# A non-local block and two Mamba passes: the last 1x1 convolution of 20 of 28 position tiles inside the second Mamba stage, z made in its own tile, GpSimd's ring with five places

## What is computed

```python
def _mamba(u, in_w, conv_w, conv_b, xp_w, dt_w, dt_b, A_log, Dp, out_w):
    x, z = jnp.split(u @ in_w.T, 2, axis=-1)          # 512 channels each
    x = silu(depthwise_conv4(x) + conv_b)
    xdbl = x @ xp_w.T                                 # dt (16), B (16), C (16)
    dt = softplus(xdbl[..., :16] @ dt_w.T + dt_b)
    h_t = exp(dt * A) * h_(t-1) + (dt * x) * B        # 16 states for each of 512 channels
    y = (sum_n h * C + x * Dp) * silu(z)
    return y @ out_w.T
y1, y2 = mamba1(x0), mamba2(x0)                       # x0: result of layer 0
out = cat_conv_w @ concat(y1, y2) + cat_conv_b + x0
```

## Time and profile before

| | us |
|---|---|
| median of 3 runs | 6042.82 (6040.0 to 6043.99) |
| the profiled execution | 6041.77 |
| its span, first to last instruction | 6040.0 |
| PE busy | 5095.7 (84%) |
| DVE busy | 5052.4 (84%) |
| POOL busy | 5066.3 (84%) |
| ACT busy | 3549.0 (59%) |
| `finish`, first matmul to end of span | 5774.2 to 6040.0 |

### The profile page before, as it was taken

How to read it: one execution, slowest core, us unless ns; L and a number is a source line. 1 busy time by engine, 2 the same in 40 slices (tenths; PEclk the granted TensorE clock), 3 DMA queues, 4 the chain that set the end, 5 groups by cost and what they waited for, 6 DMA issues and landing times. The chain is left out here.

```text
span 6040.0 us, 69966 instructions
## 1 busy us (share of the span) xinstructions
PE 5095.7 (84%) x25566; PEld 3554.5 (59%) x25566; DVE 5052.4 (84%) x3473; ACT 3549.0 (59%) x5494; POOL 5066.3 (84%) x2582
## 2 busy tenths in 40 slices
PE   6968888888888888888678888888888888888789
PEld 5836565665565566555545566655665566665544
DVE  3459999999999999999949999999999999999900
ACT  0046666666666666666546666666666666666511
...
GB/s 153 70 101 100 94 76 108 68 98 100 71 108 68 99 100 70 108 68 98 59 76 100 104 66 107 64 103 90 80 108 62 104 82 87 108 62 101 56 212 143
DMA packets 220108, 563.74 MB, mean 93 GB/s; under 512 B 27794, under 2 KB 94226, under 8 KB 218228
## 3 DMA queue, kind: packets, MB, share of 16 engines
...
## 5 line engine op out<-in xcount | busy, mean ns | idle before, releaser
L868 POOL TENSOR_TENSOR dbx<-dtx,b_all 128x896 f32<-128x896 f32 x1792 | 3695.0, 2090 | 0.2
L708 ACT ACTIVATE mamba_ps<-dt,w 128x448 f32<-128x448 f32 x3584 | 2132.4, 629 | 1555.9 <-DVE hc L820 1288.7
L813 DVE TENSOR_TENSOR_SCAN mamba_ps<-mamba_ps,dbx 128x896 f32<-128x896 f32 x1232 | 2483.2, 2016 | 211.0 <-ACT mamba_ps L708 109.7
L661 PEld LDWEIGHTS mamba_ps<-ident,hc 128*112 128x112 f32 x14336 | 1782.6, 145 | 787.9 <-issue 390.3
L661 PE MATMUL mamba_ps<-ident,hc 128*112 128x128 f32 x14336 | 2043.7, 295 | 234.3 <-POOL hc L875 141.9
L820 DVE TENSOR_TENSOR hc<-mamba_ps,c_all 128x896 f32<-128x896 f32 x1232 | 1341.6, 1089 | 137.1 <-DVE mamba_ps L813 3.4
L875 POOL TENSOR_TENSOR hc<-hc,c_all 128x896 f32<-128x896 f32 x560 | 1166.7, 2083 | 226.0 <-DVE hc L813 223.5
L813 DVE TENSOR_TENSOR_SCAN hc<-mamba_ps,dbx 128x896 f32<-128x896 f32 x560 | 1128.6, 2015 | 117.9 <-ACT mamba_ps L708 117.9
L577 PE MATMUL mamba_ps<-u,w 128*128 128x448 f32 x1792 | 880.6, 621 | 387.7 <-DVE sz L802 298.3
L577 PEld LDWEIGHTS mamba_ps<-u,w 128*128 128x128 f32 x1792 | 337.9, 209 | 643.2 <-DVE sz L802 327.3
L586 PE MATMUL mamba_ps<-x,taps 128*128 128x448 f32 (+3 forms) x1792 | 704.5, 536 | 12.0 <-ACT x L722 12.0
...
## 6 DMA issues: line engine op xcount, KB each, us to landing
b_all<-bc_scratch SPq DMA_DIRECT2D x448, 448.0 KB, 5.8
c_all<-bc_scratch SPq DMA_DIRECT2D x448, 448.0 KB, 5.1
u<-u_scratch SPq DMA_DIRECT2D x56, 448.0 KB, 7.7
y_scratch<-ytok SPq DMA_DIRECT2D x56, 448.0 KB, 3.2
src<-y_scratch SPq DMA_DIRECT2D x56, 448.0 KB, 4.6
...
u_scratch<-ub ACTq DMA_DIRECT2D x28, 448.0 KB, 8.2
src<-in_x SPq DMA_DIRECT2D x28, 448.0 KB, 6.8
```

Source lines behind the costliest of these rows:

```text
L661: ins = nc.tensor.matmul(y_ps[j % 2][:, c * 128:(c + 1) * 128], hc[g][:, e * T + c * TCH:e * T + (c + 1) * TCH], ident[:, :], start=False, ...
L708: ins = nc.scalar.activation(decay[g % 2][:, e * T:(e + 1) * T], blk(dt[t % 2], j), ACT.Exp, scale=w[:, c:c + 1])
L813: nc.vector.tensor_tensor_scan(dst, h, dbx[n % BX_RING][:, :], 0.0, ALU.mult, ALU.add).then_inc(scan_done, 1)
L868: nc.gpsimd.tensor_tensor(view(dbx[n % BX_RING], 0, [[T, 2], [1, T]]), view(dtx[t % 2], j * T, [[0, 2], [1, T]]), view(b_all, 2 * g * T, [ ...
```

## The change

The items z0 to z3 leave the front: they are made in their own tile, in slots 0 to 5, and silu of z moves from slot 3 to slot 8. The x and convolution items of the next tile move back to make room, out1's copy moves from ACT slot 16 to 15 (ahead of the decays of slot 16), y2 from PE slot 30 to 29. `dtx` becomes one buffer instead of two, with a wait on dbx, and the dbx ring has five places instead of six.

Under tiles 36 to 55 the jobs of batches 0 and 1 and six of batch 2 run, one job a tile, in two pieces of 224 columns: items fa0, fa1 (one for each output half) and fb0, fb1. The pieces share one source buffer and one result buffer. SP loads piece a after the load of u, and piece b, followed by the store of piece a, inside the loads of the next tile's rows, behind `c_all` of group 2; the store of piece b is at the end of its step. `finish` keeps eight jobs, each with its own buffers; its maps are loaded one by one and not copied.

```diff
 SCHEDULE = {
-    "x0": (0, 1), "x1": (1, 2), "c0": (3, 5), "c1": (4, 6), "y3": (6, None), "x2": (7, 8), "x3": (9, 10), "c2": (10, 11),
-    "c3": (12, 13), "out0": (13, 14), "out1": (15, 16), "y0": (16, None), "xp": (18, 19), "dt0": (19, 20), "dt1": (20, 21),
-    "dt2": (21, 22), "dt3": (22, 23), "y1": (23, None), "z0": (24, 25), "z1": (26, 27), "z2": (27, 28), "z3": (28, 29),
-    "y2": (30, None),
+    "z0": (0, 1), "z1": (1, 2), "x0": (2, 3), "x1": (3, 4), "z2": (4, 5), "z3": (5, 6), "c0": (6, 7), "y3": (6, None),
+    "c1": (8, 9), "x2": (8, 10), "x3": (10, 11), "c2": (10, 12), "c3": (12, 13), "out0": (13, 14), "out1": (15, 15),
+    "y0": (16, None), "xp": (18, 19), "dt0": (19, 20), "dt1": (20, 21), "dt2": (21, 22), "dt3": (22, 23), "y1": (23, None),
+    "fa0": (24, 25), "fa1": (25, 26), "y2": (29, None), "fb0": (30, 31), "fb1": (31, 31),
 }
-FRONT = ("x0", "x1", "c0", "c1", "x2", "x3", "c2", "c3", "xp", "dt0", "dt1", "dt2", "dt3", "z0", "z1", "z2", "z3")
+FRONT = ("x0", "x1", "c0", "c1", "x2", "x3", "c2", "c3", "xp", "dt0", "dt1", "dt2", "dt3")
 BACK = ("y3", "out0", "out1")
-SILU_Z_AT, SILU_X_AT, SOFTPLUS_AT = 3, 16, 24
-TAKE_Y_AT = {3: 3, 12: 0, 20: 1, 28: 2}
+SILU_Z_AT, SILU_X_AT, SOFTPLUS_AT = 8, 16, 24
+TAKE_Y_AT = {4: 3, 12: 0, 20: 1, 28: 2}
 GATE_AT = {7: 3, 16: 0, 24: 1, 31: 2}
 DTX_AT, LATE_DTX_AT = {29: 0, 30: 1}, {6: 2, 7: 3}
 
 
+
+FIN, FIN_FROM = T // 2, TILES + TPB + 1
+FIN_TILES = range(FIN_FROM, 2 * TILES)
+
+
+def fin_of(t):
+
+    return (t - FIN_FROM) // TPB, (t - FIN_FROM) % TPB * T
+
+
 def due(engine, n):
 
     return [name for name, at in SCHEDULE.items() if at[engine] == n]
 
 
-BX_RING, HC_RING = 6, 8
+BX_RING, HC_RING = 5, 8
 
 
 def by_pool(n):
...
-        dtx = [sb(f"dtx{p}", DB * T) for p in range(2)]
+        dtx = sb("dtx", DB * T)
...
+                    b, n0 = fin_of(t)
+                    if piece == 1:
+                        it = Item(t, "fa1")
+                        sp.wait_ge(work_ready, it.ready())
+                    elif t > FIN_FROM:
+                        it = Item(t - 1, "fb1")
+                        sp.wait_ge(work_ready, it.ready())
+                    if piece == 0 and n0 == 0:
+                        if b:
+                            it = Item(t - 1, "fb1")
+                            sp.wait_ge(work_free[it.slot], it.freed())
+                        sp.dma_start(now[:, :], k_dram[b]).then_inc(now_ready, 16)
+                        sp.wait_ge(y_stored, 16 * (TILES + TPB * (b + 1)))
+                    n0 += piece * FIN
+                    s = src[:, :].rearrange("p (k n) -> p k n", k=6)
+                    for m in range(2):
+                        sp.dma_start(s[:, 2 * m:2 * m + 2, :], y_img[m][b][:, :, n0:n0 + FIN]).then_inc(src_ready, 16)
+                    sp.dma_start(s[:, 4:6, :], x_in[b].rearrange("(k p) n -> p k n", p=128)[:, :, n0:n0 + FIN]).then_inc(src_ready, 16)
+
+                def store_out(t, piece):
+                    b, n0 = fin_of(t)
+                    n0 += piece * FIN
+                    for oc in range(2):
+                        it = Item(t, f"f{'ab'[piece]}{oc}")
+                        sp.wait_ge(work_free[it.slot], it.freed())
+                    sp.dma_start(out[b].rearrange("(k p) n -> p k n", p=128)[:, :, n0:n0 + FIN],
+                                 res[:, :].rearrange("p (k n) -> p k n", k=2)).then_inc(out_stored, 16)
+
+                def between(t):
+                    if t in FIN_TILES:
+                        load_src(t, 1)
+                        store_out(t, 0)
 
                 def spread_bc(t):
...
+                        if g == 2:
+                            between(t - 1)
...
-                        sp.wait_ge(work_ready, Item(t, FRONT[-1]).ready())
+                        sp.wait_ge(work_ready, Item(t, "z3").ready())
                         load_u(t + 2)
+                    if t == FIN_FROM:
+                        sp.dma_start(cat_t[:, :], cat_dram).then_inc(cat_ready, 16)
+                    if t in FIN_TILES:
+                        load_src(t, 0)
                     if not first(t):
                         store(t - 1)
                     if last(t):
+                        between(t)
                         store(t)
                     else:
                         spread_bc(t + 1)
+                    if t in FIN_TILES:
+                        store_out(t, 1)
                 sp.wait_ge(y_stored, 2 * 16 * TILES)
...
+                def fin(t, piece, oc):
+                    if oc == 0:
+                        if t == FIN_FROM and piece == 0:
+                            pe.wait_ge(cat_ready, 16)
+                        pe.wait_ge(now_ready, 16 * (fin_of(t)[0] + 1))
+                        pe.wait_ge(src_ready, 48 * (2 * (t - FIN_FROM) + piece + 1))
+                    b = take(Item(t, f"f{'ab'[piece]}{oc}"))
+                    for k in range(6):
+                        m = cat_t[:, k * CH + oc * 128:k * CH + (oc + 1) * 128] if k < 4 else \
+                            now[:, (k - 4) * CH + oc * 128:(k - 4) * CH + (oc + 1) * 128]
+                        ins = nc.tensor.matmul(b[:, 0:FIN], m, src[:, k * FIN:(k + 1) * FIN], start=(k == 0), stop=(k == 5))
                     ins.then_inc(work_ready, 1)
 
...
+                            elif name[0] == "z":
+                                in_proj(t, name, DIN + int(name[1]) * 128)
+                            elif name[0] == "f":
+                                if t in FIN_TILES:
+                                    fin(t, "ab".index(name[1]), int(name[2]))
...
+                def take_fin(t, piece, oc):
+                    if oc == 0:
+                        upto(act, out_stored, 16 * (2 * (t - FIN_FROM) + piece))
+                    it = Item(t, f"f{'ab'[piece]}{oc}")
+                    nc.scalar.activation(res[:, oc * FIN:(oc + 1) * FIN], take(it)[:, 0:FIN], ACT.Identity,
+                                         bias=now[:, 2 * CH + oc:2 * CH + oc + 1]).then_inc(work_free[it.slot], 1)
...
+                    d, dx = pair(dt[t % 2], h), pair(dtx, h)
                     if k % 2 == 0:
                         pool.wait_ge(softplus_ready, t + 1)
+                        upto(pool, dbx_ready, SLOTS * (t - 1) + 16 * (h + 1))
...
+    b0, n0 = fin_of(2 * TILES)
+    jobs = [(b0, i) for i in range(n0 // T, TPB)] + [(b, i) for b in range(b0 + 1, BATCH) for i in range(TPB)]
...
-                dve.wait_ge(fixed, 32)
-                for b in range(BATCH):
-                    dve.wait_ge(made, b * TPB + TPB)
-                    dve.wait_ge(taken, b * TPB + TPB)
-                    nc.vector.tensor_copy(now[:, :], maps[:, bass.ds(b * KCOLS, KCOLS)]).then_inc(now_ready, 1)
```

More of the change, by code:

```diff
@@ L490, in mambas @@
             for name in SCHEDULE:
+                if name[0] == "f" and t not in FIN_TILES:
+                    continue
                 of = t + 1 if name in FRONT else t - 1 if name in BACK else t
@@ L904, in finish @@
         ps = ctx.enter_context(nc.psum_tensor("fin_ps", [128, 8 * 512], fp32))
-        src = [sb(f"src{i}", 6 * T) for i in range(TPB)]
-        res = [sb(f"res{i}", 2 * T) for i in range(TPB)]
-        cat_t, maps, now = sb("cat_tt", 4 * CH), sb("maps", BATCH * KCOLS), sb("now", KCOLS)
-        fixed, src_ready = sem("fixed"), [sem(f"src_ready{i}") for i in range(TPB)]
-        now_ready, made, taken = sem("now_ready"), sem("made"), sem("taken")
-        stored = [sem(f"out_stored{i}") for i in range(TPB)]
+        src = [sb(f"last_src{i}", 6 * T) for i in range(len(jobs))]
+        res = [sb(f"last_res{i}", 2 * T) for i in range(len(jobs))]
+        cat_t, maps = sb("last_cat", 4 * CH), [sb(f"map{b}", KCOLS) for b in batches]
+        fixed, src_ready = sem("fixed"), [sem(f"last_ready{i}") for i in range(len(jobs))]
+        made, taken, stored = sem("made"), sem("taken"), sem("last_stored")
         y_img = y_dram.rearrange("(m b t) n f -> m b (t n f)", m=2, b=BATCH).rearrange("m b (k p n) -> m b p k n", k=2, p=128)
@@ L936, in _ @@
+                for j, (b, i) in enumerate(jobs):
+                    s = src[j][:, :].rearrange("p (k n) -> p k n", k=6)
+                    for m in range(2):
+                        sp.dma_start(s[:, 2 * m:2 * m + 2, :], y_img[m][b][:, :, i * T:(i + 1) * T]).then_inc(src_ready[j], 16)
+                    sp.dma_start(s[:, 4:6, :], x_in[b].rearrange("(k p) n -> p k n", p=128)[:, :, i * T:(i + 1) * T]).then_inc(src_ready[j], 16)
             @block.tensor
             def _(pe):
-                pe.wait_ge(fixed, 32)
@@ L939, in _ @@
-                for b in range(BATCH):
-                    pe.wait_ge(now_ready, b + 1)
-                    for i in range(TPB):
-                        pe.wait_ge(src_ready[i], b * 48 + 48)
-                        back = 4 if i >= 4 else (7 if i == 3 else 3)
-                        pe.wait_ge(taken, b * TPB + (i + 1 - back + TPB))
-                        for oc in range(2):
```

(33 more changed lines are left out.)

64 lines of the change are left out of this document (26 added, 38 removed).

## The result

The changed kernel takes 6065.95 us (median of 5 runs, 6064.14 to 6071.32), the kernel before 6042.82 beside it (5 runs, 6037.19 to 6055.3). The ratio is 1.0038 [1.0024, 1.0053]: slower by 23 us. The forecast was 6085, slower by 42. The profiled execution has a span of 6063.2, 23.2 more than before.

A forecast was written before the change was run, and what follows sets the result against it. VectorE, waiting for ScalarE's decays, sets a tile's length; the last stage is TensorE alone. 6040.0 - 186.5 - 15.7 + 125 - 4 + 84 + 14 + 25 = 6082 us of span, forecast 6085, range 5950 to 6175.

The forecast's parts named there:

- Last stage: TensorE's closing stage shrinks from 28 jobs to 8, from 261.4 to 74.9 us: 186.5 saved.
- Lead-ins: ScalarE's four z copies leave the two lead-ins, where they stood between dt and softplus: 15.7 us saved.
- Part 3: z in slots 0 to 5 makes out1 late, its copy ahead of slot 16's decays: +2.4 us a tile, 125 over 52.
- The seam: First scan (S0) of the tile after each of tiles 36 to 54, late behind fb1: 4.4 us each, 84 over 19.
- The backlog: TensorE, still owing a sum and z0 behind a seam, is 0.8 us later than elsewhere: 14 us over 18.
- Tiles 0, 27, 28, 55: These tiles lack half of the delaying items and win the 1.0 us wait at slot 4: -4 us in all.
- Queue of SP, rows of B, ring of five, one dtx: Rows queued behind the pieces on SP (bounds 0 to 3), GpSimd's five-place ring (0 to 1 a tile), single dtx: 0 us.
- Clock: TensorE at half clock for dt makes softplus late: half of the 49 us if all tiles turn long, 25.
- A: TensorE's queue is absorbed, out1 there when ScalarE comes: Part 3 and Clock 0, 5935 us, or 6010 with half; chance 0.24.
- B: Half clock spreads to all tiles, fb1 and the next tile's x0: 87 us more, 6172, slower; chance 0.18.
- C: GpSimd starves, by group 3's rows or the ring: about 6140 us, slower; chance 0.08.

The follow-up runs named there:

- Experiment 1: The changed kernel with out1's copy back in ACT slot 16, behind that slot's decays: 5963.3 us, 0.9879 of the kernel before.
- experiment 9: The changed kernel with out1 made behind y0 in slot 17 and copied in slot 18, behind silu of x: 5751.65 us, 0.9526 of the kernel before.
- experiment 5: The changed kernel without pieces (all 28 jobs in the last stage) and with six ring places: 6189.23 us, against 6185.99 with five.
- experiment 8: The kernel before the change with idle transposes for TensorE in its two waits ahead of dt: 5914.71 us, 0.9782.
- experiment 11: The changed kernel with piece b's source loaded behind c_all of group 0 and piece a stored behind group 1: 6087.66 us, 1.0084 of the kernel before.
- experiments 6 to 8: Idle transposes (8 ahead of xp, 20 ahead of dt0) in the changed kernel, 5969.55 us; that with out1 at 16 and early fb pieces, 5829.62; the kernel before, 5914.71.

## Why the prediction was right, point by point

**Last stage.** 186.5 forecast, 185.7 measured; its matmuls take 74.37, forecast 74.9. **Lead-ins**: 15.7 forecast, 10.2 + 8.3 = 18.5 measured, the second with tile 27's gain of 0.8 in it.

**Part 3, the dear one.** Forecast +2.4 a tile; by slot it is -0.97 (slot 4) + 0.19 + 0.49 + 1.88 + 0.67 (slots 9, 15, 16, 17) = 2.26 in tiles 1 to 26, and 120 us over all 52, forecast 125. out1's matmuls end at 45.7, forecast 45.4 (44.23 + 1.2), and slot 17's scan starts at 53.0 in both. The path is the one named: ScalarE idle for out1 with slot 16's decays behind it. Experiment 1 shows it by giving these decays their place back, experiment 9 by taking out1 away altogether. What the prediction read as a term of 125 us is thus real, and was avoidable.

**The seam.** Forecast 4.4, measured 4.03 (within 3.2 to 6.5). fb0 did come late and at half clock, the sum behind it ended near 0, and fb1 found full clock in all 19 seams: in the tile shown it runs from 0.0 to 2.4 after the place where S0 would have come (4443.09), forecast 0 to 2.6. **The backlog** of 0.8 behind a seam, 14 us, is the term of the sum that failed. TensorE does come late: its first convolution item starts at 14.26 in tiles 37 to 54, 0.6 behind the 13.63 of tiles 1 to 26. But nothing passes that on. x3 starts at 25.88 in both, since it waits for a copy anyway (TensorE idles 0.65 ahead of it there, 0.21 here), and out1 ends at 45.76 and 45.75; slots 15 to 17 wait as elsewhere. The prediction had this wait itself, the 1.1 of x3 and c2 in part 3, and did not take the 0.8 off it.

**Tiles 0, 27, 28, 55.** Forecast -4; tile 0 takes 2.4 more (91.8 to 94.2), tile 28 1.6 more, tile 55 0.8 less, together +3. A small term with the wrong sign. In tile 0 the waits at slots 4, 11 and 12 (1.5 together) go, and slots 9, 10, 13 and 14 wait 3.7; tile 28 is alike. Why, I did not follow.

**Queue of SP, rows of B, ring of five, one dtx.** Forecast 0 each. Among GpSimd's waits in the changed kernel there is none for b_all. Group 3's b_all, the one that the prediction watched, lands 6.0 after its issue in tiles 37 to 55 against 5.5 in tiles 2 to 27, and at least 1.6 before GpSimd's instruction that reads it starts (group 4's at least 1.2), where the prediction left about 1. The ring order of which "DMA: Bandwidth & Descriptors" of the Trainium skill speaks (section "Queues, rings and completion order") may be in that 0.5; it brought no wait. GpSimd does wait for its ring, 149.9 us in all:

```profile
POOL hc L966 <- DVE hc L903: 293.5, 170, 7.3
POOL dbx L959 <- DVE mamba_ps L903: 149.9, 95, 3.6
```

and experiment 5 shows that this is the old wait in another place. VectorE never waits for GpSimd inside the tiles. Its one such wait from 375 to 5952 us is that of the first scan of tile 28, in the lead-in:

```profile
DVE mamba_ps L903 <- POOL dbx L959: 43.2, 1, 43.2
```

**Clock.** Forecast 25 us over 52 tiles, half of "all tiles long". Slots 23 to 25 rose from 1.83 to 2.58 in tiles 1 to 26 and from 2.17 to 2.71 in tiles 29 to 35, but fell from 2.50 to 2.00 in tiles 36 to 54: 26 x 0.75 + 7 x 0.54 - 19 x 0.50 = 14. The term was 11 too large, and its sign was wrong under the pieces. Its weight was not seen either: I priced what the change would add to the half clock and left what was already there (experiment 8: 100 us of waits, and 128 us in all) as given.

**Sum.** Tiles were forecast at 125 - 4 + 84 + 14 + 25 = 244. Measured term by term they are 120 + 3 + 77 + 0 + 14 = 214, and with 13 more, nearly all of it VectorE's longer busy time, which the forecast did not have, they cost 84 + 21 + 119 + 3 = 227. The lead-ins gave 3 more. 17 + 3, and 1 less in the last stage, make the 19 us between 6085 and 6066. The mechanism and the two large terms were right; that the total is only 19 off is in part luck, since 30 us too many in the waits met 13 that were missing.

**The rivals.** A (TensorE's queue absorbed) fell: ScalarE waits 3.46 for out1. B (half clock spreads) came in small part: tiles with full clock over slots 19 to 22 went from 16 to 6 of 52. Its fb1 at half clock did not happen in the changed kernel, for a reason that experiment 11 makes visible: its condition, TensorE idle ahead of the gate, was one load away, and with it fb1 is at half clock and the kernel is 22 us slower than changed (6087.66 - 6065.95), 17 of them at the seams. C (GpSimd starves) fell, by the waits above.

**What stays open.** Why experiment 1 lifts the granted clock in some tiles only (23 tiles have it in part) and why slot 17's wait shrinks in experiment 8 (20 of its 128 us) were not followed to a cause. Which of the two groups of transposes, 8 or 20, does the work in experiments 6 to 8 was not run.
